# One product fewer in the encoder's masked sums, with the two halves of v added by GpSimd

## The reference, cut to what matters

```python
def _sierpinski_mask(S):
    i = np.arange(S)
    return jnp.asarray((np.bitwise_and(i[:, None], i[None, :]) == 0).astype(np.float32))
...
scores = jnp.einsum('bhqd,bhkd->bhqk', q, k) * scale
scores = scores * smask
a = jax.nn.softmax(scores, axis=-1)
att = jnp.einsum('bhqk,bhkd->bhqd', a, v)
```

## Time and profile before

| | us |
|---|---|
| median of 3 runs (4094.0 to 4099.04) | 4095.8 |
| the profiled execution, its own time | 4093.98 |
| its span in the trace | 4092.1 |
| busy in the span: PE | 3362.9 (82%) |
| DVE | 2512.2 (61%) |
| ACT | 1836.8 (45%) |
| POOL | 1057.8 (26%) |

### The profile page before, as it was taken

How to read it: one execution, slowest core, us unless ns; L and a number is a source line. 1 busy time by engine, 2 the same in 40 slices (tenths; PEclk the granted TensorE clock), 3 DMA queues, 4 the chain that set the end, 5 groups by cost and what they waited for, 6 DMA issues and landing times. The chain is left out here.

```text
span 4092.1 us, 68321 instructions
## 1 busy us (share of the span) xinstructions
PE 3362.9 (82%) x25711; PEld 2345.6 (57%) x25711; DVE 2512.2 (61%) x6468; ACT 1836.8 (45%) x3001; POOL 1057.8 (26%) x1362
## 2 busy tenths in 40 slices
PE   5999999999999999996768586777566659997996
PEld 3666666666666666665668254556354424444674
DVE  4865875775775875874510698886685741115663
ACT  1565565565565565664534552222232213332443
POOL 1324324324324324322454110000201320004321
PEclk8999999999999999998789786998776669997997
DMA  5423534434433534430155100000000000004430
GB/s 134 117 71 98 116 73 99 115 73 100 115 73 97 117 74 99 116 91 1 41 160 181 47 1 0 1 0 1 6 1 5 1 29 0 0 0 110 94 81 26
DMA packets 177020, 262.06 MB, mean 64 GB/s; under 512 B 19950, under 2 KB 149230, under 8 KB 159694
## 3 DMA queue, kind: packets, MB, share of 16 engines
q1 hardware_dynamic: 152494, 140.93, 12.3%
q10 hardware_dynamic: 19656, 107.37, 12.0%
q0 software_dynamic: 4544, 9.38, 0.7%
HBM read 184.67 MB, written 72.19 MB: 63 GB/s over the span
## 5 line engine op out<-in xcount | busy, mean ns | idle before, releaser
L870 DVE TENSOR_REDUCE enc_mx<-psum 128x2 f32<-128x512 f32 (+1 forms) x1152 | 755.6, 685 | 155.7 <-PE psum L550 153.0
L1036 ACT ACTIVATE enc_e<-psum 128x1024 f32<-128x1024 f32 (+1 forms) x768 | 580.3, 808 | 400.4 <-PE psum L571 309.3
L550 PE MATMUL psum<-enc_ks,enc_qs 80*128 80x128 bf16 (+1 forms) x3072 | 459.5, 253 | 69.4 <-DVE enc_mx L870 55.2
L571 PE MATMUL psum<-enc_qs,enc_ks 83*128 83x256 bf16 (+1 forms) x3072 | 380.3, 249 | 29.6 <-DMA enc_qs<-enc_turned_max 21.0
L550 PEld LDWEIGHTS psum<-enc_ks,enc_qs 80*128 80x128 bf16 x3072 | 221.6, 99 | 190.5 <-DVE enc_mx L870 110.4
L584 PE MATMUL psum<-enc_e,enc_v 128*32 128x256 f32 (+1 forms) x6144 | 330.7, 333 | 0.0
L571 PEld LDWEIGHTS psum<-enc_qs,enc_ks 83*128 83x128 bf16 x3072 | 258.2, 98 | 67.8 <-DMA enc_qs<-enc_turned_max 21.4
L584 PEld LDWEIGHTS psum<-enc_e,enc_v 128*32 128x32 f32 x6144 | 160.6, 109 | 161.3 <-ACT enc_e L1036 50.8
L2781 PE MATMUL psum<-ter_h,par_s 128*128 128x512 f32 x512 | 224.9, 593 | 2.4 <-DVE ter_h L2832 1.6
L640 PE MATMUL psum<-par_layerr,enc_hidden 128*128 128x128 f32 x1536 | 191.6, 279 | 16.2 <-DVE enc_n_rows L915 16.2
L640 PEld LDWEIGHTS psum<-par_layerr,enc_hidden 128*128 128x128 f32 x1536 | 182.4, 194 | 26.9 <-DVE enc_n_rows L915 21.2
(11 more groups left out here) (531 smaller groups left out, 7235.3 us busy)
## 6 DMA issues: line engine op xcount, KB each, us to landing
enc_qs<-q_pieces ACTq DMA_DIRECT2D x234, 192.0 KB
enc_ks<-k_pieces ACTq DMA_DIRECT2D x234, 192.0 KB
k_pieces<-enc_pieces SPq DMA_DIRECT2D x240, 128.0 KB, 2.0
moe_wb<-moe_w SPq DMA_DIRECT2D x39, 512.0 KB
q_pieces<-enc_pieces SPq DMA_DIRECT2D x144, 128.0 KB, 2.0
enc_qs<-q_pieces SPq DMA_DIRECT2D x54, 192.0 KB
enc_ks<-k_pieces SPq DMA_DIRECT2D x54, 192.0 KB
rope_qs<-q_pieces ACTq DMA_DIRECT2D x39, 192.0 KB
```

The costliest lines, as they stand in the source:

```text
L550: last = T_.matmul(p1[f % 2][:, i * kw:(i + 1) * kw], qs[0:KEYED, slot, h, j * P:(j + 1) * P], ks[0:KEYED, slot, h, 0:kw], start=True, sto ...
L571: last = T_.matmul(p2[ch][:, g], ks[0:SCORED, slot, 4 * T + g, ch * P:(ch + 1) * P], qs[0:SCORED, slot, 4 * T + g, 0:n], start=True, stop= ...
L870: V.tensor_reduce(mx[:, u % 2, j * HEADS + h0:j * HEADS + h0 + n], p1[f % 2].rearrange("p (h k) -> p h k", h=n), AX_X, ALU.max)\
L1036: A.activation(e_of(T, ch), p2[ch], ACT.Exp, scale=HD ** -0.5).then_inc(s_e, 1)
```

## The change

`masked_sum` multiplies, for the first half of the queries, the mask once with the sum of the two halves of v, so three products a sequence in place of four. The sum, `v_both`, is a new buffer of 4 slots by 144 numbers of float32 a partition. GpSimd computes it in `add_halves`, one addition of 128 partitions by 288 numbers for a group (two sequences), both inputs in SBUF. TensorE waits for the new semaphore `s_both` in place of `s_v`.

```diff
+            def add_halves(layer, nxt, g):
+
+                pool.wait_ge(s_v, at(layer, GROUPS, g + 1, nxt))
+                s = SEQ_G * g % SLOTS
+                G.tensor_tensor(v_both[:, s:s + SEQ_G], v[:, s:s + SEQ_G, 0, :, 0:VW], v[:, s:s + SEQ_G, 1, :, 0:VW], ALU.add).then_inc(s_both, 1)
...
             first(0, 0, 1)
+            add_halves(0, 0, 0)
             cut_maxima(0, 0, 0)
...
-                    elif m:
-                        N1.root(pool, at(layer, GROUPS, m - 1))
+                    else:
+                        if m:
+                            N1.root(pool, at(layer, GROUPS, m - 1))
+                        if m + 1 < GROUPS:
+                            add_halves(layer, 0, m + 1)
...
                     if g == 5:
                         residual1(layer, GROUPS - 1)
+                        if not last:
+                            add_halves(layer, 1, 0)
...
             def masked_sum(layer, u):
-                pe.wait_ge(s_v, at(layer, GROUPS, u // 2 + 1))
-                for j in range(JT):
-                    for ch in range(JT):
-                        last = T_.matmul(misc[:, j * HEADS * VW:(j + 1) * HEADS * VW].rearrange("p (h v) -> p h v", v=VW), zero[:, ch, j * P:(j + 1) * P],
-                                         v[:, u % SLOTS, ch, :, 0:VW], start=(ch == 0), stop=(ch == 1))
-                last.then_inc(s_u, 1)
+                pe.wait_ge(s_both, at(layer, GROUPS, u // 2 + 1))
+                rows = [misc[:, j * HEADS * VW:(j + 1) * HEADS * VW].rearrange("p (h v) -> p h v", v=VW) for j in range(JT)]
+                T_.matmul(rows[0], zero[:, 0, 0:P], v_both[:, u % SLOTS], start=True, stop=True)
+                T_.matmul(rows[1], zero[:, 0, P:2 * P], v[:, u % SLOTS, 0, :, 0:VW], start=True, stop=False)
+                T_.matmul(rows[1], zero[:, 1, P:2 * P], v[:, u % SLOTS, 1, :, 0:VW], start=False, stop=True).then_inc(s_u, 1)
```

More of the change, by code:

```diff
@@ L269, in encoder @@
         v = sb("v", [P, SLOTS, JT, HEADS, 32])
+        v_both = sb("v_both", [P, SLOTS, HEADS, VW])
         mx = sb("mx", [P, 2, JT * HEADS])
@@ L288, in encoder @@
         s_stored, s_loaded = [sem(f"pieces_stored{i}") for i in range(2)], [sem(f"pieces_loaded{i}") for i in range(SLOTS)]
-        s_vp, s_v = sem("vproj_ready"), sem("v_moved")
+        s_vp, s_v, s_both = sem("vproj_ready"), sem("v_moved"), sem("v_halves_added")
         s_p1, s_mx = sem("scores_ready"), sem("max_taken")
```

## The result

| | before | changed |
|---|---|---|
| median of 4 runs of each, one chip | 4097.42 us (4094.0 to 4099.2) | 4136.34 us (4131.9 to 4138.9) |
| ratio, 95% interval | | 1.0087 [1.0073, 1.0102] |
| profiled execution, its own time / span | 4093.98 / 4092.1 us | 4138.03 / 4136.2 us |
| mean granted clock of TensorE | 0.901 | 0.886 |

The change makes the kernel slower by 0.87%, some 36 us in the interval's middle and 39 by the medians. The forecast was 4097.5, and its range ended at 4109. Most of its steps are found in the trace; the sum lacked a term as large as its largest one.

A forecast was written before the change was run, and what follows sets the result against it. TensorE was taken as the bound up to a masked sum, then VectorE in the third and fourth quarter. 4093.98 - 19.5 (products) + 21.2 (stalls) = 4095.7 profiled, 4097.5 us for the median; range 4074 to 4109.

The forecast's parts named there:

- What the addition costs VectorE: Attention, odd sequences: GpSimd's addition holds up VectorE's L897 multiplication, 0.59 us late each, passed to TensorE in full.
- A product is worth 0.25 us: TensorE's masked sums: each product dropped saves 0.25 us, arriving in full in the odd sequences.
- 0.10 us in the even sequences: Even sequences u = 2 to 10: ScalarE's last load issue holds the exponential, so only 0.10 us is gained.
- all 19.5 us: Gain from fewer products over six layers: 3.25 us a layer, 19.5 us in sum.
- The addition takes 0.79 us: GpSimd's addition of 128 by 288 takes 0.79 us, with ends at 0.45 and 1.27.
- The second rival: GpSimd wins and its addition is long: at 1.27 us the 36 stalls cost 38.5 us, total 4114.8; chance 0.10.
- It starts 0.99 us behind the root's start and 0.06 ahead of L897, 36 times; GpSimd wins: Odd sequences u = 3 to 13: the addition starts at 774.45, L897 at 774.51, so L897 must wait.
- The first rival: VectorE wins the race for the 36 additions, GpSimd pays in spare time, the gain stays: 4076.3; chance 0.26.
- 21.2 us for the stalls: 36 multiplications of VectorE, each 0.59 us late behind GpSimd's addition, cost 21.2 us.
- The third rival: VectorE or ScalarE absorbs the products' gain in more places: 0.10 us in all 96 sums, total 4107.4; chance 0.08.
- Busy time of the masked sums 24 to 30 us less: Sign on TensorE: 576 instructions in place of 768, and 24 to 30 us less busy time.
- The range: 8 times in 10, from the first rival to half way to the second: 4074 to 4109 us.

The follow-up runs named there:

- e12: e1 run again on one chip with e9, e10 and e11: three products, addition ahead of the root; ratio to the kernel before 0.9959.
- e9: e1 with the four products of before in each masked sum, the addition's result not used; ratio to the kernel before 1.0004.
- e1: Changed kernel with GpSimd's addition issued ahead of the inverse root instead of behind it; ratio to the kernel before 0.9962, 15.6 us faster.
- e4: Changed kernel with a small GpSimd addition (128 by 32) between root and big addition, u = 3 to 13; ratio to the kernel before 0.9968.
- e6: e1 plus an unused VectorE addition of 128 by 528 ahead of the multiplication in the 36 places; ratio to the kernel before 1.0073.
- e5: Changed kernel plus eight unused bf16 identity products on TensorE ahead of the products that wait for VectorE's maximum; ratio to the kernel before 1.0025.
- e10: The changed kernel run again on one chip with e9, e11 and e12: three products, addition behind the root; ratio to the kernel before 1.009.
- e11: e2 run again on one chip with e9, e10 and e12: four products, addition behind the root; ratio to the kernel before 1.0109.
- e2: Changed kernel, additions where they are, but the four products of before in each masked sum; ratio to the kernel before 1.0095.
- e7: e1 plus an unused VectorE addition of 128 by 212 ahead of the multiplication in the 36 places; ratio to the kernel before 1.0008.
- e3: Changed kernel without GpSimd's additions, first product reading only v's first half, so the result is not the reference's; ratio to the kernel before 0.9963.

## Why the prediction was wrong

The step that failed is the last of "What the addition costs VectorE": "so it costs 0.59 us in full". It took a wait that TensorE is given to cost its own length. It has a second price, the speed of what follows. The earlier trace rows has TensorE's products behind 0.81 us of waiting at full speed, and I did not ask whether they would still be at 1.4. The runs showed this in its place: in 21 of the 36 places the clock fell to half behind the wait, 25.4 us that the sum had at nothing. That is 25 of the 39 us between forecast and measurement.

- **A product is worth 0.25 us:** right. 0.25 in the even sequence's timeline, 0.26 in the odd intervals.
- **0.10 us in the even sequences:** the mechanism is right, the size low. The exponential follows the load issue, and the intervals went from 15.72 to 15.63 in some places and to 15.55 in most, 0.09 and 0.17. Forecast for all 19.5 us, measured without the stall 18.5 (e12 against e9) and 15.6 (e1), each to some 6 us.
- **The addition takes 0.79 us:** 0.83. The second rival, a long one, is wrong.
- **It starts 0.99 us behind the root's start and 0.06 ahead of L897, 36 times; GpSimd wins:** right in every number. The first rival (4076.3) is wrong; e4 shows how narrowly, since 0.14 us behind in place of 0.06 ahead makes VectorE win, and the time come out 13 us under before (the rival had 19.5).
- **21.2 us for the stalls:** the stall itself is right, 36 x 0.63 = 22.7. Its consequence isn't: 25.4 us of falls were not in the sum. e6 shows that lateness alone brings them, e5 that work in the wait takes most away.
- **The third rival (4107.4), the gain lost:** not in the way it said. In part the clock takes it (e10 and e11).
- **Busy time of the masked sums 24 to 30 us less:** nearly. The 576 instructions stand in three lines now, and their groups of 46.8 + 41.8 + 41.1 us can't be added, since the lines overlap. Taken together they are busy for 97.8 us against 119.6 in the earlier trace rows, 21.8 less, and in e1 for 94.4, 25.2 less.
- **The range:** it was to end half way to the second rival. Half way from 4097.5 to 4114.8 is 4106, not 4109.

The sum, made again: 4095.8 - 18.5 + 22.7 + 25.4 = 4125.4, against 4136.3 measured. Some 11 us remain, 1.6 of them because the compared runs of before have a median of 4097.4. In the profiled executions the first three intervals of the layers, where the clock falls in every kernel, were 4.1 us longer after than before where the products should have made them some 4 shorter; the clock was low there for 45.1 us against 28.7, which at half speed is up to 8 us. That it is the change which brings these is not shown: in e10, the same kernel, it is 25.1 us. 2 us more are between the layers' attention parts, in the feed-forward work, and 4 from the last masked sum to the end, not explained.

The waits alone would have hidden the loss. From 77 to 1880 us of the span, TensorE's waits for VectorE's maxima grew by 23 us (from 52.8), and those for `enc_n_normed` shrank by 7:

```profile
PE psum L563 <- DVE enc_mx L882: 75.7, 66, 2.4
...
PE psum L190 <- DVE enc_n_normed L182: 5.3, 15, 0.4
```

A TensorE at half clock is busy, not waiting. The 15 waits in place of 36 at L190 are in the 15 places without a fall; in the 21 with one TensorE came late itself.

## What to carry to other kernels

Before a wait is lengthened on the engine that is the bound, look at what runs behind it and at the granted clock there: here 0.63 us more of waiting cost 1.3 us a time, (22.7 + 25.4) / 36. An independent operation of GpSimd that reads SBUF should not be issued where it starts just ahead of a VectorE operation on the critical path; the same addition was free in the idle time before the root. Where a wait can't be shortened, filler work on TensorE may be cheaper than the fall of its clock: in e5 it gave back some 25 of 36 us.

## What the runs showed of the hardware

- Behind a single wait of 1.36 to 1.45 us in a full stretch of work the granted clock fell in 16 to 23 of 36 places (five profiles: changed, e2, e6, e10, e11), behind 1.03 to 1.10 us in 4 (e7), behind 0.93 to 1.00 in 1 (e5), behind 0.74 to 0.84 in none (before, e1, e3, e4, e9, e12). It is not pure chance: in the changed kernel it fell at u = 5 in all six layers and at u = 13 in one, and in e10 in six and two. What tells the places apart was not found.
- The fall came at different distances from the restart: in the changed kernel from 0.08 us ahead of it to 1.53 us behind it, in the middle 0.9. The clock stayed low for 3.4 us each time, once for 6.8. One fall of 3.4 us cost 0.9 to 1.25 us.
- A lead of 0.06 us decided between 0.92 and 0.29 us for L909, all 36 times. The Trainium skill's "SBUF — State Buffer", section "Who interferes with whom", calls the shared ports an exclusive lock; the trace agrees, down to this lead. The price for the one that comes second is short when the first is short: 0.33 us behind the spacer of 0.24 (e4).
